# Macaron block (two feed-forward halves around a state-space layer): the shift of the layer norm, one VectorE instruction, split into a negation on VectorE and a multiplication on GpSimd

## The reference

```
def _layernorm(x, axis=-1, eps=1e-05):
    m = jnp.mean(x, axis=axis, keepdims=True)
    v = jnp.var(x, axis=axis, keepdims=True)
    return (x - m) / jnp.sqrt(v + eps)
...
    x = x + 0.5 * _L0_ffn_ref(_layernorm(x, axis=-1), ...)     # silu(x Wg) * (x Wu), then Wd; 768 hidden
    x = x + _L0_attn_ref(_layernorm(x, axis=-1), ...)          # conv, gates, scan over 16 states, C, D, W_out
    x = x + 0.5 * _L0_ffn_ref(_layernorm(x, axis=-1), ...)
```

## Time and profile before

| | |
|---|---|
| median of 3 runs | 2379.62 us |
| the profiled execution | 2370.51 us |
| its span, first to last instruction | 2368.6 us |
| TensorE, VectorE busy | 2228.1 us (94%), 2213.7 us (93%) |
| ScalarE, GpSimd busy | 2066.3 us (87%), 2063.0 us (87%) |
| mean granted TensorE clock | 0.965 of full |
| one row of the batch in the middle | 137.2 to 140.9 us between the first scans of two rows |

### The profile page before, as it was taken

The page is one execution under the profiler, slowest core; times in us unless marked ns, Lnnn a source line. Parts: engine busy times, 40 slices in busy tenths (PEclk is TensorE's granted clock), DMA queues, the critical chain, the costliest instruction groups (busy, mean ns, idle before and its releaser), DMA issues. The chain is left out here.

```text
span 2368.6 us, 28880 instructions
## 1 busy us (share of the span) xinstructions
PE 2228.1 (94%) x9220; PEld 1349.8 (57%) x9220; DVE 2213.7 (93%) x2454; ACT 2066.3 (87%) x2952; POOL 2063.0 (87%) x1286
## 2 busy tenths in 40 slices
PE   6987999999999999999999999999999999999488
PEld 3453656556565655656655565655656565565256
DVE  2499999999999999999999999999999999999992
ACT  4788999999999999989989998998999999898672
POOL 2588999999899999989899998999999999999873
PEclk9997999999999999999999999999999999999789
DMA  2022344444343443434343343444434343433220
GB/s 88 30 78 68 138 134 135 143 134 142 120 149 133 135 142 134 136 126 151 126 140 137 125 151 123 145 138 132 141 134 143 125 152 134 134 125 121 76 72 27
DMA packets 112029, 291.22 MB, mean 123 GB/s; under 512 B 11201, under 2 KB 45314, under 8 KB 111874
## 3 DMA queue, kind: packets, MB, share of 16 engines
q1 hardware_dynamic: 111874, 289.35, 36.6%
HBM read 271.49 MB, written 17.83 MB: 122 GB/s over the span
## 5 line engine op out<-in xcount | busy, mean ns | idle before, releaser
L1016 POOL TENSOR_TENSOR acc<-acc,ring 128x1024 f32<-128x1024 f32 x512 | 1208.7, 2361 | 107.3 <-DVE ring L1206 91.6
L1170 DVE TENSOR_TENSOR_SCAN g_bank<-du_bank,ring 128x1024 f32<-128x1024 f32 (+1 forms) x512 | 1098.7, 2151 | 8.7 <-ACT ring L941 4.5
L691 PE MATMUL work<-wd_t,hid 128*128 128x256 f32 x3072 | 687.9, 382 | 8.7 <-DVE hid L1123 4.1
L1206 DVE SCALAR_TENSOR_TENSOR ring<-g_bank,inv_a,ring 128x1024 f32<-128x1024 f32 (+1 forms) x576 | 661.7, 1154 | 6.6
L691 PEld LDWEIGHTS work<-wd_t,hid 128*128 128x128 f32 x3072 | 585.2, 191 | 107.8 <-issue 16.5
L941 ACT ACTIVATE ring<-dt,a_coef 128x1024 f32<-128x1024 f32 (+1 forms) x576 | 574.0, 1045 | 8.7 <-DVE g_bank L1170 6.4
L759 ACT ACT_TABLE_LOAD x315 | 404.1, 1283 | 5.6
L679 PE MATMUL work<-xt_hi,wg_t 128*128 128x512 f16 x768 | 296.0, 385 | 27.7 <-ACT sil L823 20.0
L679 PE MATMUL work<-xt_hi,wu_t 128*128 128x512 f16 x768 | 303.9, 396 | 8.6 <-ACT sil L823 6.1
L984 POOL TENSOR_TENSOR hid<-hid,sil 128x512 f32<-128x512 f32 x192 | 244.1, 1276 | 69.1 <-ACT hid L831 55.5
L679 PE MATMUL work<-xt_lo,wu_t 128*128 128x512 f16 x768 | 302.7, 394 | 0.0
(11 more groups left out here) (96 smaller groups left out, 2755.4 us busy)
## 6 DMA issues: line engine op xcount, KB each, us to landing
ring<-c_rows SPq DMA_DIRECT2D x448, 512.0 KB, 3.6
ring<-c_rows SPq DMA_DIRECT2D x64, 256.0 KB, 3.1
x_in<-L_attn_x SPq DMA_DIRECT2D x30, 512.0 KB, 4.9
out<-x_fin SPq DMA_DIRECT2D x30, 512.0 KB, 4.5
x_fin<-L_attn_x SPq DMA_DIRECT2D x2, 512.0 KB, 7.0
c_rows<-params SPq DMA_DIRECT2D x32, 32.0 KB, 3.3
out<-x_in SPq DMA_DIRECT2D x2, 512.0 KB, 2.9
ring<-L_ffn_w_gate SPq DMA_DIRECT2D x1, 768.0 KB, 5.7
```

The costliest lines, as they stand in the source:

```text
L691: last = pe.matmul(dst[:, j * E:(j + 1) * E], hid[:, K.unit[f, bt, c, m] % HIDS, t:t + P], wd_t[:, m, :], start=(m == 0), stop=(m == HM - 1))
L1016: nc.gpsimd.tensor_tensor(v, v, shaped(bt, cg[:, K.number[ev[1:]] % TERMS, :]), ALU.add).then_inc(S["summed"], 1)
L1170: scan = nc.vector.tensor_tensor_scan(g, du_h, d_h, first[0], ALU.add, ALU.mult)
L1206: nc.vector.scalar_tensor_tensor(v, g, inv_a[:, h, s:s + 1], c_row, ALU.mult, ALU.mult).then_inc(S["weighted"], 1)
```

## The change

The step `ls` goes from VectorE's queue and from the tables. Its work is done in two places. VectorE, right after the four `bn_aggr` of step `ln`, waits for them and writes minus the mean into `shift` (new semaphore `turned`). GpSimd, right after the power of step `lr`, waits for its own result and for `turned`, and multiplies `shift` by `rstd` in place. ScalarE's step `lx` waits for that product. All other due times in the tables are as before.

```diff
@@ row_events
-            for kind in ("ln", "lr", "ls", "lx", "T", "Te") + (("Ts", "Tl") if f != 2 else ()):
+            for kind in ("ln", "lr", "lx", "T", "Te") + (("Ts", "Tl") if f != 2 else ()):
...
@@ increments
         if kind == "ln":
-            return [("meanvar", 1)]
+            return [("meanvar", 1), ("turned", 1)]
+        if kind == "lr":
+            return [("rstd", 2), ("shift", 1)]
...
@@ scalar, lx
-                    wait(act, "shift", ("ls",) + ev[1:])
+                    wait(act, "shift", ("lr",) + ev[1:])
...
@@ gpsimd, lr
                     nc.gpsimd.tensor_tensor(r, r, minus_half[:], ALU.pow).then_inc(S["rstd"], 1)
+                    wait(pool, "rstd", ev)
+                    wait(pool, "turned", ("ln",) + ev[1:])
+                    nc.gpsimd.tensor_tensor(shift[:, slot, :], shift[:, slot, :], r, ALU.mult).then_inc(S["shift"], 1)
...
@@ vector, ln
                         last.then_inc(S["meanvar"], 1)
-                    elif kind == "ls":
-                        slot = K.at["shift", ev][1] % 2
-                        wait(dve, "rstd", ("lr",) + ev[1:])
-                        nc.vector.scalar_tensor_tensor(shift[:, slot, :], meanvar[:, slot, :, 0], -1.0, rstd[:, slot, :],
-                                                       ALU.mult, ALU.mult).then_inc(S["shift"], 1)
+                        wait(dve, "meanvar", ev)
+                        nc.vector.tensor_scalar(shift[:, slot, :], meanvar[:, slot, :, 0], -1.0, None,
+                                                ALU.mult).then_inc(S["turned"], 1)
```

More of the change, by code:

```diff
@@ L164 @@
     "lr1": [-88.835, -51.814],
-    "ls1": [-72.986, -40.117],
     "lx1": [-79.454, -56.766],
@@ L173 @@
     "lr2": [-13.99, -4.702],
-    "ls2": [-21.49, 0.928],
     "lx2": [-21.851, 1.35],
@@ L403, in increments @@
                "d": "du", "da": "sp_exp", "dl": "sp_ln", "dp": "sp_sum", "si": "silu",
-               "hp": "product", "rp": "mid_added", "ra": "fin_added", "lr": "rstd", "ls": "shift", "Ts": "lowered", "lx": "normed"}
+               "hp": "product", "rp": "mid_added", "ra": "fin_added", "Ts": "lowered", "lx": "normed"}
         if kind in one:
-            return [(one[kind], {"da": 2, "dp": 3, "dl": 3, "lr": 2, "Ts": EH}.get(kind, 1))]
+            return [(one[kind], {"da": 2, "dp": 3, "dl": 3, "Ts": EH}.get(kind, 1))]
         if kind == "ld":
@@ L955, in _ @@
                     _, f, bt, c = ev
-                    slot = K.at["rstd", ev][1] // 2 % 2
+                    slot = K.at["shift", ev][1] % 2
                     was = K.prev["rstd", ev]
```

## The result

The changed kernel takes 2406.46 us (median of 4 runs, 2404.45 to 2409.79), the kernel before 2378.26 us beside it: ratio 1.0123, interval 1.0108 to 1.0138. It is 28 us slower where 11 were forecast, and ends 1.5 us above the range. The profiled execution took 2404.45 us (span 2402.3), against 2370.51 before. In the middle of the program a row of the batch lasts 142.0 us on average from its first scan to that of the next, against 139.6 before.

The account below looks back on a forecast made before the run. VectorE, busy 137.8 of 139.5 us a row, was taken as the bound; 59.7 us added less 43, 1 and 5 gave +10.7, so 2370.5 became about 2381.5 profiled and 2390 us median, range 2349 to 2405.

Parts of the forecast that it names:

- the long form: VectorE's shift product L1113 at 2.30 to 2.35 us, waiting for GpSimd; price 2.3 us, a 139.5 against a 137.2 us row.
- the removed 43: VectorE time saved by dropping L1113: 49.7 us, less 0.07 us each under the neighbour's end and 6.0 us of power waits.
- the stretch at 0.60: TensorE's granted clock behind the long shift, 0.60 (partly 1.2 GHz), where the row without it has 1.00 (2.4 GHz).
- The negation waits for GpSimd like L1113: New VectorE negation behind the aggregations: taken to be blocked by running GpSimd instructions, between 0.14 and 2.35 us each.
- the doubled rate: VectorE's one-source TENSOR_SCALAR takes 0.48 ns per further element against L1206's 1.06, so it must have two SBUF streams open.
- rival 1: Faster: the negation does not wait for GpSimd, all near 0.14 us; 20 to 34 us off, 2350 us; chance 0.23.
- Third unit 29.9 us, second unit 11.5, 96 x 0.17 for the rest: Negation's cost on VectorE: blocked 15 x 1.99 us and 14 times 0.82 us at two units; 16.3 us unblocked for all 96.
- ScalarE's cover of 5 us: VectorE's wait of 0.36 us a row for ScalarE disappears as VectorE comes later: 14 x 0.36 = 5 us off.
- GpSimd 206 ns and hidden: GpSimd's 96 new multiplications at 206 ns plus 0.08 us wait, 27 us in all, fit into its 10 us idle per row.
- The sum, +10.7: VectorE's net: 59.7 added - 43 removed - 1 - 5 = 10.7 us, some 0.7 us in a row.
- Rival 2: Slower by more: the stall behind the third unit delays ScalarE, then TensorE; 14 us on top, 2404 us; chance 0.13.
- Rival 3: No change: the moved stall costs less than the old one, one us less per row cancels 10.7; 2378 us; chance 0.22.

Follow-up runs that it names:

- u1_busy_old: `r2_all_gpsimd` plus two added VectorE reductions of about 2.1 us in 15 rows, at the first norm's second chunk: 2372.66 us, ratio 0.9978.
- r2_all_gpsimd: The changed kernel with the negation given to GpSimd as well, so VectorE has no instruction for shift: 2359.37 us, ratio 0.9913.
- r1_one_stream: The changed kernel with the negation replaced by a reduction over an axis of length one, same place and wait: 2364.41 us, ratio 0.9937.
- t1_after_xmid_first: The changed kernel with ScalarE's copy x_mid before the last of eight exponentials: 2402.92 us, ratio 1.0101; same edit on the kernel before: 2375.58 us, ratio 0.9990.

## Why the prediction was wrong

- *What the row pays for the long form is the difference of the two rows, 2.3 us.* **This is the step that failed.** It made the long shift's removal worth its length. At this place VectorE's lost time costs half or less (15 us for 32.9 in `u1_busy_old`, 0.4 of 2.19 us in rows of equal clock); before pays 20.7 us for the removed 43. The sum's own 43 us of VectorE time were right. The two rows differ in two things at once, the stall and the granted clock, 0.99 and 1.00. `r2_all_gpsimd`, with no stall at all, has rows of 138.8 us at 0.99 and of 137.3 at 1.00: some 1.5 of the 2.3 us go with the clock, and 0.7 are the stall's. The prediction read the stretch at 0.60 as the stall's own doing; it stands in the rows of `r2_all_gpsimd` too. The short row was one row alone: `r1_one_stream`, with no stall in any, has rows from 136.7 to 140.2 us. That VectorE has no room, read from 137.8 busy of 139.5 us, is the same error: its held time is in the busy time, and without it a row of 140.22 us holds 134.85 [the window of `r2_all_gpsimd`].
- *The negation waits for GpSimd like L1113.* Right, and reached from the doubled rate. The reduction and the one-element instructions show the other side; rival 1's condition was not met, and where it is met its 2350 is 14 us too low for the same wrong price.
- *Third unit 29.9 us, second unit 11.5, 96 x 0.17 for the rest.* The places, their count and their cause were right. Sizes were slightly low: 2.30 for 2.13 us, because a subtraction of GpSimd (L1026, until 1006.32) delayed its sum, so that it began 0.09 us ahead of the negation; and 0.17 for 0.14 us unheld. Measured with 0.03 us ahead of each, 59.2 + 96 x 0.03 = 62.1 us for 59.7.
- *ScalarE's cover of 5 us.* Right: VectorE's wait for ScalarE's `ring` is absorbed (4.5 us before, 0.5 after).
- *GpSimd 206 ns and hidden.* Right: 203 ns, 19.5 us, and `r2_all_gpsimd`, with 96 more such instructions, is not slower for them.
- *The sum, +10.7.* Of VectorE's 62.1 us added 50 are paid, of the 43 removed 21: +29 us by ratios, where 28 were measured and 10.7 forecast. In rows at a granted clock of 0.99 the change costs 1.6 us, 23 us in 14 rows, for the 0.7 us a row of the forecast.
- *Rival 2 (2404 us, 0.13)* named what took place: ScalarE waits 2.83 us behind the third unit, 50.6 us in all. It was put aside because TensorE's present loss would go with the old stall. Part of it did, the matmuls' wait for `x_fin` (8.6 us before, 0.8 after); the stretch at the low clock stayed, as it stands in rows without a stall too. TensorE comes later all the same: VectorE's wait for it rose from 60.0 to 75.9 us. The waits for `x_mid` are real (23.5 us of the weight loads, 11.7 of the matmuls at the same places), but `t1_after_xmid_first` shows that they are not the price. The mean granted clock hardly moved between the two kernels (0.963 for 0.965). That 2404 us comes within 3 us of the measured time is in part luck, since its sum adds 14 us to a forecast that holds the wrong price.
- *Rival 3* priced the moved stall below the old one; it is the other way round.

## What to carry to other kernels

Where two engines are both nearly full, a stall on one is worth what the next meeting with the other leaves of it: look how far ahead of a wait for the other engine it stands, and who is queued behind it. Ten to twenty us ahead half of it or more was free here; 56 us ahead and with a third engine waiting for it, little was. A single odd row is no price: put rows of the same granted clock side by side before the difference is given to an instruction. And busy time that holds waiting inside is no proof of a full engine: keep a variant with every such wait taken out as the floor to measure from.

## What the runs showed of the hardware

A VectorE `tensor_scalar` of four strided f32 elements per partition, with one source, waits for GpSimd's running instruction as one with two sources does (at the old place 2.33 against 2.35 us, 547 against 518 ns on average). A reduction of the same four elements does not (157 ns), nor do four instructions of one element each (146 ns, 0.34 us for the four beside GpSimd's sums), nor reductions of 1536 and 384 elements (1.72 and 0.54 us at both places). Splitting the held instruction into four was thus faster than the whole (0.34 us for 2.30).

TensorE's granted clock fell, to as little as 0.50 over 5 us, at one place of nearly every row of the middle, 115 to 125 us behind its first scan, with stalls and without, and a row in which it fell was 1.5 or 2.9 us longer than one in which it did not (138.8 and 140.2 for 137.3 us in `r2_all_gpsimd`).
